# Two wide attentions as one stream of slots, with each group of the input prepared beside the slots before its first use

## The chip, the cores and the metric

The kernel runs on one core of a Trainium2 chip. The core has a matrix engine (TensorE, PE in the rows; PEld is its weight load), three engines for elementwise work (VectorE or DVE, ScalarE or ACT, GpSimd or POOL), SyncE (SP), which issues transfers here, and 16 DMA engines. The metric is the device time of one execution in microseconds, from three runs, and beside it one profiled execution with a trace of all instructions.

## The reference

The input x has 32 x 64 = 2048 tokens of 256 values, and so has the context. Four layers follow one another. The first one, cut to what matters here:

```python
def _cross_attention(q_in, kv_in, wq, bq, wk, bk, wv, bv, wo, bo, bias_k, bias_v):   # H = 16 heads, K = 128
    qh, kh, vh = (q_in @ wq + bq), (kv_in @ wk + bk), (kv_in @ wv + bv)      # each split into heads
    kh = concatenate([kh, bias_k]); vh = concatenate([vh, bias_v])            # one learned key and value
    weights = softmax(einsum('bqhk,bthk->bhqt', qh, kh) / sqrt(K))
    return einsum('bhqt,bthk->bqhk', weights, vh).reshape(...) @ wo + bo

h = layer_norm(x, ln1_scale, ln1_offset);  x = x + _cross_attention(h, ctx, ...1)
h = layer_norm(x, ln2_scale, ln2_offset);  x = x + _cross_attention(h, ctx, ...2)
h = layer_norm(x, ln_mlp_scale, ln_mlp_offset)
x = x + gelu(h @ w_fc1 + b_fc1) @ w_fc2 + b_fc2                               # F = 1024
```

A sequence has 64 queries and 64 keys. The layers after it (a grouped attention, an instance normalised one, a decoder layer with an MLP) are the same code before and after.

## The kernel before

All products of this layer are made in pairs of float32r parts: an operand is split into a high part (a copy rounded to float32r) and a low part (operand minus high part), and `product` (L98 to L102) makes three matmuls, high x high, high x low and low x high.

The tokens are 16 tiles of 128 rows (`NT`), in four groups of four tiles, 512 tokens (`NG`, `GT`, `GN`). `chip.x` holds the rows. `h_hi` and `h_lo` hold the normalised input with the features on the partitions (turned), `ctx_hi` and `ctx_lo` the context.

The stages run one after another, with a barrier between them:

- `load` (L110) brings the context and x in on SP's queue, turns the context on TensorE, splits it (ScalarE, GpSimd), and measures both on VectorE.
- `wide_attention` runs twice (n = 1, 2). It first calls `turn_input` (L186), which for all four groups inverts the spread on GpSimd (L92, L94), normalises the rows on VectorE (L277), turns them (L238), scales them and splits them (L256, L259 on ScalarE, L270 on VectorE). Biases are turned into columns beside it (L364, L369), and `spread_v` is set up for the product of the learned values (L375, L377).
- Then come the slots. One slot is one head for one group: 8 passes of two heads (`HP`) and four groups, 64 slots. A slot n does on TensorE: turn the weights of slot n-1 (L522), project q, context product of slot n-2 (L542), project k and v, for odd slots the output product of a group into `o_ps`, then the scores (L588). ScalarE empties q, k, v, makes the exponential and the high part of the context product (L621 to L648), VectorE makes the softmax and the low part (L667 to L688) and adds `o_ps` to x (L718), GpSimd splits the next pass's weights (L468 to L487). The last pass is written out, the others are one loop body.
- The learned value of each head enters through `learned_weight` (one column a head), which is turned in one go at the end (L528), and multiplied by `value_rows` for all 16 tiles (L567, L706). `value_rows` comes from a product over all heads, `values` (L512), half of it before slot 0 and half behind it.
- The MLP of this layer, `dense_mlp` with tag l0m, loads and splits its weights beside its own `turn_input`, then runs 4 groups of 8 chunks (`FC`): the first layer's chunk f+2, then the second layer's chunk f. From group 1 on it also turns the finished rows for the next layer (L853).

## Time and profile before

| what | value |
|---|---|
| median of 3 runs | 1855.43 us (1854.35 to 1855.84) |
| the profiled execution, its own time | 1856.37 us |
| its span, first to last instruction | 1854.4 us |
| mean granted TensorE clock | 0.959 of full speed |
| busy: TensorE, VectorE, ScalarE, GpSimd | 92, 51, 55, 26% |

### The profile page before, as it was taken

To read this page: it belongs to the slowest core of one execution; us is meant where nothing else is said; L and a number is where in the kernel's file an instruction comes from. 1 tells how busy PE (TensorE), PEld (TensorE's weight loads), DVE (VectorE), ACT (ScalarE), POOL (GpSimd) and SP (SyncE) were. 2 spreads that over 40 slices of the span, in tenths; PEclk is the share of its full clock that TensorE was granted. 3 is DMA by queue.
4 is the path that set the end of the run, shared out by engine and by line. 5 is a ranking of instruction groups with operands and counts; after the bars stand their busy time and mean duration, and the time that the engine had idled before them with its cause. 6 is when DMAs were issued, how large, how long until landed. Compare 5 with 4: busy or idle time off the path is not lost. (4 is left out here: it accounts for less than half of the span.)

```text
span 1854.4 us, 36201 instructions
## 1 busy us (share of the span) xinstructions
PE 1713.5 (92%) x14357; PEld 1458.7 (79%) x14357; DVE 950.7 (51%) x2107; ACT 1012.1 (55%) x1949; POOL 481.3 (26%) x554
## 2 busy tenths in 40 slices
PE   5999999999978999999999869999989889997599
PEld 4888898888867898888888758866766567776598
DVE  6444444444454444444444473467859847668433
ACT  5455555554524555555455434457748857776444
POOL 5000000000012000000000021147764558876411
PEclk7999999999988999999999979989989989999799
DMA  5000000000002000000000020030010000001001
GB/s 160 24 23 9 13 23 23 23 0 23 1 21 72 1 23 23 23 0 23 23 23 0 1 77 1 1 101 2 2 22 2 1 6 2 1 7 36 1 12 34
DMA packets 58100, 39.87 MB, mean 22 GB/s; under 512 B 14693, under 2 KB 57238, under 8 KB 58006
## 3 DMA queue, kind: packets, MB, share of 16 engines
q1 hardware_dynamic: 58006, 38.57, 7.1%
q8 instruction: 65, 1.06, 0.2%
q14 instruction: 29, 0.24, 0.0%
HBM read 36.46 MB, written 2.10 MB: 21 GB/s over the span
## 5 line engine op out<-in xcount | busy, mean ns | idle before, releaser
L679 DVE TENSOR_TENSOR l0a_c_lo<-l0a_c_ps,l0a_c_hi 128x512 fp32r<-128x512 f32 x128 | 88.6, 692 | 267.3 <-ACT l0a_c_hi L633 267.3
L621 ACT ACTIVATE l0a_weight_t<-l0a_t_ps 64x256 f32<-64x256 f32 x256 | 96.9, 378 | 230.7 <-PE l0a_t_ps L522 229.2
L718 DVE TENSOR_TENSOR x<-l0a_o_ps,x 128x1024 f32<-128x1024 f32 x64 | 78.4, 1225 | 202.7 <-PE l0a_o_ps L102 202.7
L542 PEld LDWEIGHTS l0a_c_ps<-l0a_weight_t,l0a_v 128*128 128x128 f32 x1024 | 135.3, 193 | 14.3 <-ACT l0a_weight_t L621 3.0
L468 POOL COPY l0a_head_bias<-l0a_bias_cols 128x2 f32 (+1 forms) x32 | 6.9, 214 | 531.2 <-DVE l0a_logit L672 531.2
L100 PE MATMUL l0a_o_ps<-l0a_wo_hi,l0a_c_hi 128*128 128x256 f32 x512 | 144.2, 282 | 0.0
L101 PE MATMUL l0a_o_ps<-l0a_wo_lo,l0a_c_hi 128*128 128x256 f32 x512 | 143.8, 281 | 0.0
L102 PE MATMUL l0a_o_ps<-l0a_wo_hi,l0a_c_lo 128*128 128x256 f32 x512 | 143.7, 281 | 0.0
L102 PE MATMUL l0a_v_ps<-l0a_wv_hi,ctx_lo 128*128 128x256 f32 x512 | 143.6, 280 | 0.0
L100 PE MATMUL l0a_v_ps<-l0a_wv_hi,ctx_hi 128*128 128x256 f32 x512 | 143.6, 280 | 0.0
L101 PE MATMUL l0a_v_ps<-l0a_wv_lo,ctx_hi 128*128 128x256 f32 x512 | 143.0, 279 | 0.0
L542 PE MATMUL l0a_c_ps<-l0a_weight_t,l0a_v 128*128 128x128 f32 x1024 | 137.1, 277 | 1.7 <-ACT l0a_weight_t L621 1.7
L630 ACT ACTIVATE l0a_q<-l0a_q_ps,l0a_head_bias 128x512 f32<-128x512 f32 x128 | 88.0, 687 | 90.0 <-PE l0a_q_ps L102 89.3
L639 ACT ACTIVATE l0a_k<-l0a_k_ps,l0a_head_bias 128x512 f32<-128x512 f32 x128 | 88.1, 689 | 63.8 <-PE l0a_k_ps L102 63.8
L648 ACT ACTIVATE l0a_v<-l0a_v_ps 128x512 f32<-128x512 f32 x128 | 76.5, 598 | 77.1 <-PE l0a_v_ps L102 77.1
L100 PE MATMUL l0a_q_ps<-h_hi,l0a_w_hi 128*128 128x512 f32 x256 | 112.4, 439 | 3.5 <-POOL l0a_w_lo L473 3.5
L100 PE MATMUL l0a_k_ps<-ctx_hi,l0a_w_hi 128*128 128x512 f32 x256 | 111.3, 435 | 0.0
L102 PE MATMUL l0a_k_ps<-ctx_hi,l0a_w_lo 128*128 128x512 f32 x256 | 101.2, 395 | 0.0
L102 PE MATMUL l0a_q_ps<-h_hi,l0a_w_lo 128*128 128x512 f32 x256 | 101.1, 395 | 0.0
L101 PE MATMUL l0a_q_ps<-h_lo,l0a_w_hi 128*128 128x512 f32 x256 | 100.9, 394 | 0.0
L101 PE MATMUL l0a_k_ps<-ctx_lo,l0a_w_hi 128*128 128x512 f32 x256 | 100.9, 394 | 0.0
L101 PEld LDWEIGHTS l0a_v_ps<-l0a_wv_lo,ctx_hi 128*128 128x128 f32 x512 | 96.0, 187 | 6.0
(429 smaller groups left out, 4869.5 us busy)
## 6 DMA issues: line engine op xcount, KB each, us to landing
l0a_raw<-in_L_xattn_wq_dram SPq DMA_DIRECT2D x32, 128.0 KB, 2.2
l0a_raw<-in_L_xattn_wk_dram SPq DMA_DIRECT2D x32, 128.0 KB, 2.3
l0a_raw_v<-in_L_xattn_wv_dram SPq DMA_DIRECT2D x16, 256.0 KB, 3.0
l0a_raw_o<-in_L_xattn_wo_dram SPq DMA_DIRECT2D x32, 128.0 KB, 2.7
l0a_wo_all<-in_L_xattn_wo_dram SPq DMA_DIRECT2D x2, 2048.0 KB, 8.2
ctx_rows<-in_ctx_dram SPq DMA_DIRECT2D x4, 512.0 KB, 5.9
x<-in_x_dram SPq DMA_DIRECT2D x4, 512.0 KB, 9.8
l3a_room<-in_L_xattn_w_fc_dram SPq DMA_DIRECT2D x2, 1024.0 KB, 6.4
```

The costliest lines, as they stand in the source:

```text
L100: pe.matmul(out, wh, mh, start=start, stop=False)
L101: pe.matmul(out, wh, ml, start=False, stop=False)
L102: return pe.matmul(out, wl, mh, start=False, stop=stop)
L468: pool.tensor_copy(head_bias[p][:], bias_cols[:, BQ:BK + 1, bass.ds(i * HP + p, 1)] .rearrange("p a b -> p (a b)"))
L542: last = pe.matmul(by_tile[:, m, b, :, :], v[(j - HP) // HP % 2][:, m * HB + b, p * K:(p + 1) * K], weight_t[:, m, b, :, :].rearrange("p a ...
L621: last = act.activation(weight_t[half, :, :, a, :], t_ps[half, 0:GT // 2 * P] .rearrange("p (m b q) -> p m b q", b=HB, q=SEQ), ACT.Copy)
L630: act.activation(q[:], q_ps[:], ACT.Identity, bias=head_bias[p][:, 0:1]).then_inc(q_done, 1)
L639: act.activation(k[p][:, :, 0:SEQ], k_ps[:].rearrange("p (b k) -> p b k", k=SEQ), ACT.Identity, bias=head_bias[p][:, 1:2]).then_inc(k_done, 1)
L648: act.activation(v[j // HP % 2][:, p * GT // HP:(p + 1) * GT // HP, :] .rearrange("p t k -> p (t k)"), v_ps[:], ACT.Copy).then_inc(v_done, 1)
L679: dve.tensor_tensor(c[p][1][:], c_ps[:], c[p][0][:].bitcast(F32), ALU.subtract).then_inc(c_lo, 1)
L718: dve.tensor_tensor(chip.x[:, rows, :], o_ps[:], chip.x[:, rows, :], ALU.add).then_inc(added, 1)
```

## The change

`load`, the two `wide_attention` calls and their `turn_input` become one function, `wide_attentions`, with one stream of 128 slots over both attentions. Numbered over both, S = 0 to 127, `passes` writes out S = 0 to 9, loops over passes 1 to 6, writes out the two passes around the seam (S = 58 to 73), loops again and writes out the last.

- x of group 0 and the weights go on SP's queue, the context and x of groups 1 to 3 on ScalarE's. Only group 0 of x and groups 0 and 1 of the context are turned ahead of slot 0. Groups 2 and 3 of the context are turned in slots 0, 2 and 3.
- `TURNS` says at the end of which slot a group of the input is turned (S = 0, 2, 4 for the first attention, 62, 64, 66, 68 for the second, 126 for the MLP's group 0), into `o_ps`. VectorE measures it two slots ahead, GpSimd normalises it one slot ahead, ScalarE and VectorE empty it one slot later and GpSimd makes the low part. Its first use is two slots later.
- The second attention's slots follow the first one's. The product of the learned values is made at the end of slots 8 and 72 in one piece, and `keep_values` one slot later; the learned weights of a group are turned with its last weights and multiplied in its last output product (four fp32 matmuls into `o_ps`).
- The first MLP's weights, biases and gains are fetched on SP's queue during the attentions, behind the second attention's value weights and ahead of pass 2's weights. In the MLP they are split in eight quarters behind the first chunks (`BEHIND`), and its groups 1 to 3 of the input are measured, normalised, turned and split in chunks of the groups ahead (`ENTRY`).
- The stage of the MLP's `turn_input` is gone. `dense_mlp` for the last layer is as before.

The diff, cut to its core:

```diff
-def load(chip):
-def turn_input(chip, tag, scale=None, offset=None, beside=None, bare=False):
-def wide_attention(chip, tag, n):
+def wide_attentions(chip, buffer, gain, mlp):
+    LAST = ATT * PASSES - 1
+    TURNS = {0: 1, 2: 2, 4: 3, **{(PASSES - 1) * ITEMS + 6 + HP * g: NG + g for g in range(NG)}, LAST * ITEMS + 6: 2 * NG}
+    VALUES = {ITEMS: 0, (PASSES + 1) * ITEMS: 1}
+    SPREAD = {HP * HP: 0, ITEMS + 1: 1}
...
+        half_banks = [o_ps[:, HP * x:HP * x + HP, :].rearrange("p t n -> p (t n)") for x in range(CH)]
...
+        def passes(engine, slots):
+            slots(0, 0, True, False, False)
+            slots(0, 1, True, True, False)
+            for j in range(2, ITEMS + 2):
+                slots(0, j, True, True, True)
+            with engine.Fori(1, PASSES - 1) as i:
+                for j in range(2, ITEMS + 2):
+                    slots(i, j, True, True, True)
+            for i in (PASSES - 1, PASSES):
+                for j in range(2, ITEMS + 2):
+                    slots(i, j, True, True, True)
+            with engine.Fori(PASSES + 1, LAST) as i:
+                for j in range(2, ITEMS + 2):
+                    slots(i, j, True, True, True, 1)
+            for j in range(2, ITEMS + 2):
+                slots(LAST, j, j < ITEMS, j <= ITEMS, True)
...
+                def normalise(n):
+                    invert(n)
+                    pool.wait_ge(norm_done, n + 1)
+                    pool.wait_ge(x_turned, n * CH)
+                    for t in range(GT):
+                        at = n % NG * GT + t
+                        pool.tensor_scalar(rows[:, t, :], chip.x[:, at, :], chip.x_moments[:, at, 0:1], norm_inverse[:, t:t + 1],
+                                           ALU.subtract, ALU.mult).then_inc(rows_done, 1)
...
+                    if S is not None and S - 1 in TURNS:
+                        m = TURNS[S - 1]
+                        for ch in range(CH):
+                            pool.wait_ge(x_whole_done, CH * m + ch + 1)
+                            pool.tensor_tensor(chip.h_lo[:, ch, group_columns(m % NG)], whole[:, ch, :],
+                                               chip.h_hi[:, ch, group_columns(m % NG)].bitcast(F32), ALU.subtract).then_inc(x_lo_done, 1)
...
+                        for t in range(GT):
+                            if ending is not None:
+                                last = pe.matmul(o_ps[:, t, :], weights_t[:], value_rows[:, t, :], start=False, stop=True)
...
+                    if S in TURNS:
+                        m = TURNS[S]
+                        if S == 0:
+                            pe.wait_ge(cols_done, 1)
+                        elif S == 2:
+                            pe.wait_ge(x_whole_done, CH * m)
+                        else:
+                            pe.wait_ge(added, outputs_before(S))
+                        turn_rows(m, half_banks)
...
+                act.dma_start(ctx_rows[:, group_rows(0), :], ctx_dram[:, group_rows(0), :]).then_inc(rows_in[0], 16)
+                for x in range(2):
+                    act.dma_start(gain[:, 0, x, :], columns(norms[0][x]), allow_slow_non_contiguous=True).then_inc(gain_in[0], 16)
+                for g in range(1, NG):
+                    act.dma_start(ctx_rows[:, group_rows(g), :], ctx_dram[:, group_rows(g), :]).then_inc(rows_in[g], 16)
+                    act.dma_start(chip.x[:, group_rows(g), :], x_dram[:, group_rows(g), :]).then_inc(x_in[g], 16)
+                for ch in range(CH):
+                    take_context(0, ch)
+                split_w(0, 0)
+                for ch in range(CH):
+                    take_context(1, ch)
+                take_rows(0, first_banks)
+                split_w(0, 1)
+                split_wv(0)
...
+                dve.wait_ge(x_in[0], 16)
+                measure_group(0)
+                for ch in range(CH):
+                    rest_of_context(0, ch)
+                normalise(0)
+                take_biases(0)
...
-def dense_mlp(chip, tag, scale, offset, w1, b1, w2, b2, function, prepared=None, out=None, room=None, turn=None):
+def dense_mlp(chip, tag, function, prepared, out=None, turn=None, entry=None):
+    ENTRY = {0: 3, 1: 1, 2: 1} if entry is not None else {}
...
+            quarters = [quarters[i] for i in (0, 2, 1, 4, 3, 6, 5, 7)]
+            BEHIND = (-1, -1, -1, 0, 1, 2, 3, 4)
+            FIRST_LAYER, SECOND_LAYER = (1, 2, 4, 6), (3, 5, 7, 8)
...
+                    if entry is not None and f == 0 and g > 0:
+                        pe.wait_ge(x_lo_done, CH * g)
+                    if entry is not None and g == 0 and f % QUARTER == 0:
+                        pe.wait_ge(w_lo_done, FIRST_LAYER[f // QUARTER])
```

## Rows read from the trace of the kernel before

**Rows 1.** The page, busy time of TensorE: us, share, instructions, then the other engines.

```profile
PE 1713.5 (92%) x14357; PEld 1458.7 (79%) x14357; DVE 950.7 (51%) x2107; ACT 1012.1 (55%) x1949; POOL 481.3 (26%) x554
```

**Rows 2.** Busy time by stretch: length, each engine's, PEclk, DMA share, GB/s.

```profile
60.00:514.00 454.00, 452.24 (x3720) 405.40 (x3716) 192.27 (x457) 234.26 (x448) 32.31 (x50) 1.00 0.06 16
523.74:573.19 49.45, 30.91 (x138) 25.33 (x134) 32.47 (x85) 15.09 (x25) 11.99 (x19) 0.72 0.22 65
1056.19:1101.16 44.97, 24.89 (x117) 20.41 (x114) 33.03 (x77) 13.98 (x24) 9.16 (x10) 0.70 0.16 50
0.00:40.73 40.73, 20.81 (x86) 17.55 (x86) 28.44 (x98) 21.41 (x35) 26.17 (x37) 0.75 0.58 182
```

**Rows 3.** Timeline of PE, first slots: start, us, what, records.

```profile
45.84 3.72 PE L512 MATMUL l0a_o_ps<-l0a_wo_all,l0a_spread_v 128*128 128x256 f32 x16
49.21 0.58 PE L100 MATMUL l0a_q_ps<-h_hi,l0a_w_hi 128*128 128x512 f32 x1
...
54.31 0.44 PE L522 MATMUL l0a_t_ps<-ident,l0a_weight 128*128 128x128 f32 x2
...
60.41 0.44 PE L522 MATMUL l0a_t_ps<-ident,l0a_weight 128*128 128x128 f32 x2
...
69.35 0.44 PE L522 MATMUL l0a_t_ps<-ident,l0a_weight 128*128 128x128 f32 x2
```

**Rows 4.** Timeline of PE, between the two attentions.

```profile
538.91 1.03 PE L567 MATMUL l0a_k_ps<-l0a_value_rows,l0a_weights_t 128*128 128x256 f32 x4
539.78 1.03 PE L567 MATMUL l0a_v_ps<-l0a_value_rows,l0a_weights_t 128*128 128x256 f32 x4
...
586.77 0.44 PE L522 MATMUL l0a_t_ps<-ident,l0a_weight 128*128 128x128 f32 x2
```

**Rows 5.** Timeline of PE, first MLP.

```profile
1111.16 0.40 PE L100 MATMUL l0m_hidden_ps<-h_hi,l0m_w_hi 128*128 128x512 f32 x1
...
1146.80 1.03 PE L853 MATMUL l0m_turn_ps<-ident,x 128*128 128x128 f32 x8
1147.59 0.47 PE L100 MATMUL l0m_hidden_ps<-h_hi,l0m_w_hi 128*128 128x512 f32 x1
```

**Rows 6.** Timeline of DVE, start and end of the attentions.

```profile
4.54 1.41 DVE L178 BATCH_NORM_STATS2 ctx_stats<-ctx_rows 128x6 f32<-128x256 f32 x4 [4.54 <-DMA ctx_rows<-in_ctx_dram]
...
36.51 1.34 DVE L657 TENSOR_TENSOR l0a_wv_lo<-l0a_raw_v,l0a_wv_hi 128x512 fp32r<-128x512 f32 x1 [2.02 <-ACT l0a_wv_hi L608]
...
53.12 1.77 DVE L698 TENSOR_TENSOR l0a_value_rows<-l0a_o_ps,l0a_bo_rows 32x256 f32<-32x256 f32 x4
...
59.33 0.16 DVE L688 TENSOR_TENSOR l0a_learned_weight<-l0a_expd,l0a_inverse 128x4 f32 x1
...
1065.41 0.69 DVE L679 TENSOR_TENSOR l0a_c_lo<-l0a_c_ps,l0a_c_hi 128x512 fp32r<-128x512 f32 x1 [4.33 <-ACT l0a_c_hi L633]
...
1079.14 1.23 DVE L718 TENSOR_TENSOR x<-l0a_o_ps,x 128x1024 f32<-128x1024 f32 x1 [0.38 <-PE l0a_o_ps L102]
1080.40 1.41 DVE L76 BATCH_NORM_STATS2 x_stats<-x 128x6 f32<-128x256 f32 x4
1082.87 1.17 DVE L83 BATCH_NORM_AGGREGATE x_moments<-x_stats 128x2 f32<-128x6 f32 x16 [1.07 <-PEq L65]
```

**Rows 7.** Groups by line: busy us, mean ns, idle before (whole span, then 0:110).

```profile
L473 POOL TENSOR_TENSOR l0a_w_lo<-l0a_raw,l0a_w_hi 128x512 fp32r<-128x512 f32 x32 | 40.8, 1274 | 73.2 <-ACT l0a_w_hi L603 73.2
...
L2281 POOL TENSOR_SCALAR l_normed<-l3a_room,ctx_moments,ctx_inverse 128x256 f32<-128x256 f32 x14 | 17.4, 1246 | 23.0 <-PE l_conv_ps L2226 23.0
...
L277 DVE TENSOR_SCALAR l0a1h_rows<-x,x_moments,l0a1h_inverse 128x256 f32<-128x256 f32 x16 | 8.2, 576 | 0.9 <-POOL l0a1h_inverse L94 0.7
...
L256 ACT ACTIVATE h_hi<-l0a1h_turned,l0a1h_gain 128x512 fp32r<-128x512 f32 x8 | 6.3, 788 | 7.7 <-PE l0a1h_turned L238 7.7
...
L94 POOL TENSOR_TENSOR l0a1h_inverse<-l0a1h_spread,minus_half 128x4 f32<-128x4 f32 x4 | 4.8, 1196 | 0.3
```

**Rows 8.** Timeline of SP's DMA issues, window 7:9.2: start, us of the issue.

```profile
6.56 2.52 SPq L133 DMA_DIRECT2D x<-in_x_dram  x1
```

More of the change, by code:

```diff
@@ new lines, in _ @@
+                next_pass(1)
+                fetch_pass(0, [(HP + p) * K for p in range(HP)])
+                sp.wait_ge(values_done, 1)
+                fetch_values(1)
+                sp.wait_ge(ctx_turned, CH * NG)
+                sp.wait_ge(ctx_gathered, NG)
+                mlp["sync"](sp)
+                with sp.Fori(2, PASSES) as i:
+                    starts = [sp.snap((i * HP + p) * K) for p in range(HP)]
+                    ends, count = sp.snap(i * HP), sp.snap(i * 1)
+                    sp.wait_ge(w_split, ends)
+                    sp.wait_ge(wv_split, count)
+                    sp.wait_ge(wo_split, count)
+                    fetch_pass(0, starts)
@@ L177, in _, with measure_group @@
+                def measure_group(m):
+                    g = m % NG
+                    for t in range(GT):
+                        measure(chip, dve, g * GT + t).then_inc(measured, 1)
+                    dve.wait_ge(measured, GT * (m + 1))
                     for t in range(g * GT, (g + 1) * GT):
-                        dve.bn_stats(stats[:, t, :], rows[:, t, :]).then_inc(stats_done, 1)
+                        last = dve.bn_aggr(chip.x_moments[:, t, :], chip.x_stats[:, t, :])
+                    last.then_inc(gathered, 1)
@@ new lines, in normalise, with take_whole @@
+                def normalise(m):
+                    dve.wait_ge(norm_done, m + 1)
+                    if m > 0:
+                        dve.wait_ge(x_turned, CH * m)
+                    for t in range(GT):
+                        at = m * GT + t
+                        dve.tensor_scalar(rows[:, t, :], chip.x[:, at, :], chip.x_moments[:, at, 0:1], norm_inverse[:, t:t + 1],
+                                          ALU.subtract, ALU.mult).then_inc(rows_done, 1)
+                def take_whole(m, ch, bank):
+                    norm = m // NG
+                    dve.wait_ge(x_hi_done, CH * m + ch + 1)
+                    if m > 0:
+                        dve.wait_ge(x_lo_done, CH * (m - 1) + ch + 1)
+                    dve.tensor_scalar(whole[:, ch, :], bank[:], gain[:, norm, 0, ch:ch + 1], gain[:, norm, 1, ch:ch + 1],
+                                      ALU.mult, ALU.add).then_inc(x_whole_done, 1)
@@ L191, in turn_input @@
+                split_wv(0)
+                dve.wait_ge(x_in[1], 16)
+                measure_group(1)
+                normalise(1)
+                dve.wait_ge(zeroed, 4)
+                passes(dve, slots)
+    chip.end_stage()
+def dense_mlp(chip, tag, function, prepared, out=None, turn=None, entry=None):
     nc = chip.nc
-    scaled_norm = scale is not None
-    norm = scaled_norm or bare
-    beside = beside or {}
+    LEAD = 2
+    ENTRY = {0: 3, 1: 1, 2: 1} if entry is not None else {}
@@ L781, in dense_mlp @@
-        if not prepared:
-            with ExitStack() as before:
-                prepare(before)
+            w_hi_done, w_lo_done = sem("w_hi_done"), sem("w_lo_done")
+            QUARTER = 2
+            quarters = []
+            for start in range(0, FC, QUARTER):
+                cols, own = slice(start * P, (start + QUARTER) * P), slice(start, start + QUARTER)
+                quarters += [(raw1[:, :, cols], w1_hi[:, :, cols], w1_lo[:, :, cols]), (raw2[:, own, :], w2_hi[:, own, :], w2_lo[:, own, :])]
@@ L845, in first, with turn_entry @@
                     last.then_inc(hidden_made, 1)
+                def turn_entry(n):
+                    if n >= 2:
+                        pe.wait_ge(turned_lo, CH * (n - 1))
+                    for c in range(CH):
+                        for j in range(GT):
+                            if c == 0:
+                                pe.wait_ge(rows_done, n * GT + j + 1)
+                            last = pe.transpose(turn_ps[:, c, j * P:(j + 1) * P], rows[n % 2][:, j, c * P:(c + 1) * P], chip.ident[:])
+                        last.then_inc(x_turned, 1)
                 def turn_rows(g):
@@ L857, in group @@
                     for f in range(FC):
+                        if entry is not None and ENTRY.get(g) == f:
+                            turn_entry(g)
                         if turn and f == 5 and g > 0:
```

1183 lines of the change are left out of this document (600 added, 583 removed).

## The prediction

> **What bounds the kernel now.** I read the page first: TensorE is busy for 92% of the span [rows 1], so outside its own work there are some 140 us to be had. Where they lie I read from the busy time by stretch. In 454 us in the midst of the first attention TensorE is busy for 452.24, at a granted clock of 1.00; in the three stretches around the attentions it is busy for 20.81 of 40.73, 30.91 of 49.45 and 24.89 of 44.97 us, at clocks of 0.75, 0.72 and 0.70 [rows 2]. What looks busy there is partly slow: at the lower of the two clock levels a matmul takes twice its time. So the attention slots are bound by TensorE, and the three stretches by chains over the other engines. The change fills the stretches with slots.
>
> The timeline of TensorE then gives the unit. A slot is one head for one group of 512 tokens. An even slot takes 60.41 - 54.31 = 6.10 us, an odd one (with the output product) 69.35 - 60.41 = 8.94, a pair 15.04 [rows 3]. Counted in slots over both attentions (S), S=2 starts at 54.31, S=64 would start at 523.74 and S=128 at 1056.19, where the second and third stretch begin [rows 2, 3]; S=66 (slot 2 of the second attention) starts at 586.77 [rows 4], chunk 1 of the MLP at 1111.16 [rows 5]. I compare before and after at these marks.
>
> **Prices used.** A turn of one group (8 transposes), warm: 1147.59 - 1146.80 = 0.79 us [rows 5]. Learned product: four records, that is two matmuls, are 539.78 - 538.91 = 0.87 us apart, so 0.43 a matmul, 1.74 for a group's four; with its one more transpose (0.1) 1.84 [rows 4]. Values product: half of it takes 49.21 - 45.84 = 3.37 us, all of it 6.74 [rows 3].
>
> **Stretch 1, start to S=2.** Before, nothing useful starts until everything is loaded, measured, normalised, turned and split. After, only group 0 is. The chain: x of group 0 and the first context rows land at about 5.5 us (two 512 KB transfers share what one had, whose first use is at 4.5 [rows 6]). ScalarE is the question, since it now issues nine DMAs, seven of them of 512 KB, before its first activation. On SP the last of eight such issues was held until 6.56 + 2.52 = 9.08 us, an issue that lasted 2.52 us where half a microsecond is what one of these takes unheld [rows 8]; the queue takes some four large transfers and then holds its issuer. Three of ScalarE's seven must land first, beside 1.5 MB on SP, 3 MB in all. At SP's rate, (eight less four held) x 0.5 MB in 9.08 - 2.2 us, at least 300 GB/s, ScalarE is free at 10.5 us. Bounds: 5.5 (never held) and 14.3 (held until all is in).
> From there: two context copies of ScalarE 1.0 (two thirds of the 0.79 of its scaled 128x512 pass, an estimate), VectorE's two rests 1.3, normalise 4 x 0.53 (16 take 8.2 us busy), turn at the lower clock 1.8 of which 0.7 is behind the last row, ScalarE's two 128x512 of 0.79, VectorE's whole and low parts, four of about 0.7 [rows 6, 7]: 10.5 + 1.0 + 0.7 + 2.1 + 0.7 + 1.3 + 2.5 = 18.8 us for the first q. Slot 0 is half at the lower clock, with two turns 8.3 us, slot 1 is 5.1 and waits 0.4 for the context of group 2: S=2 at 32.6, against 54.31. That is 21.7 us less (bounds 18 to 26).
> Of what is moved into slots there are two more turns of x and one of context, 2.4; the values, 6.74; and slot 9 waits for the kept values: VectorE does them after the weights, which are ready 5.0 us into a slot (the learned column ends the series), in 1.77 us [rows 6], against TensorE's wish for o_ps at 5.6: 1.2. Together 10.3. **Net -11.4 us.**
>
> **Stretch 2, S=64 to S=66.** Before 586.77 - 523.74 = 63.03 us. After: one pair 15.04, values and their wait 7.9, four turns 3.2, four learned products 7.4 (in slots 59 to 65): 33.5. **Net -29.5 us.**
>
> **Stretch 3, S=128 to MLP chunk 1.** Before 1111.16 - 1056.19 = 54.97 us. After, the drain keeps its first part, to c_lo at 1065.41 + 0.69 [rows 6], 0.6 earlier as three learned transposes are gone. Then 24 output matmuls and one learned product, 4.6 us warm and up to 9 at the lower level; the stretch's clock of 0.70 [rows 2] says partly: 6.4. The add is 1.23, and from the end of the last statistics, which are gone, to the next stage's first aggregation are 1082.87 - 1081.81 = 1.1 [rows 6]. New stage at 1074.4. A weight quarter (128x512) has its high part from ScalarE in some 0.7 and its low part from VectorE in 0.7: first hidden product at 1075.9, then 12 matmuls mostly at the lower clock (4.6), 1.4 for chunk 2's, 1.4 for the first output product: chunk 1 at 1083.2 on before's axis, 28.0 earlier. Back: three learned products and one turn inside the slots 6.3, three turns in the MLP 2.4, and 1.0 for VectorE in chunks 2 to 4 (a chunk is 2.8 us; low, weight quarter, and four statistics with their aggregation are 0.7 + 0.7 + 1.7 = 3.1, against some 2.7 us of lead; bounds 0 to 4). **Net -18.3 us.**
>
> **What is costed at nothing.** *GpSimd* now normalises: a 128x256 tensor_scalar takes 1.246 us there, the pow 1.2, a 128x512 subtraction 1.27 [rows 7]. A turn costs it 0.23 + 1.2 + 4 x 1.25 = 6.4 and later 2.5. In an odd slot it ends the low parts about 5.0 us in, and the next normalisation 6.4 later, 2.5 us into the even slot; TensorE turns there from 5.4 on. So 2.9 us of slack. In slot 64 it also has the second head's weights, ready 6.4 us in, needed at 6.9: half a microsecond. *ScalarE* gets 1.3 us in slots S+1 and copies a learned tile: all are odd slots of 8.9 us; q and k are done by 5.0, and the scores ask for them after 8. *VectorE* ends a measuring even slot 0.7 late, and the exponential waits behind c_hi anyway. *SP*: 4 MB of values and MLP weights go ahead of pass 2's weights, 12 to 14 us; from slot 9 to their use in slot 15 are 45 us. Late next, if its cover goes, is the turn, and with it q of the next slot.
> The row shows a subtraction of two SBUF operands on VectorE of 1.34 us beside a GpSimd one, where 0.69 is usual for this shape [rows 6, 7]. In this case's stream only the weights' 0.43 us product has two SBUF inputs; a held one would be late by up to 1.25, on nine turns 11 us; by the time at which GpSimd is at work (2.5 to 11.4 us after an odd slot's start) it falls in odd slots, whose 3 us of spare hold it. The Trainium skill, "SBUF — State Buffer", "Who interferes with whom", has a VectorE instruction with two SBUF inputs wait out a GpSimd instruction that reads SBUF, for its whole length. By that rule, the trace agrees: 1.34 against 0.69. By it the sum would be 4 us less of a gain, in the MLP, where the low parts of chunks 1 to 4 run beside GpSimd's normalisation.
>
> **Sum.** -11.4 - 29.5 - 18.3 = -59.2. The profiled execution took 1856.4 us, 2.0 beyond its span, and 0.9 over the median of 1855.4. 1856.4 - 59.2 = 1797.2; by the median 1796.2. I predict 1797. Bounds: start -4 to +4, drain clock -2 to +2, MLP -1 to +4, weights' product 0 to +11.
>
> **Rivals.**
> 1. *GpSimd comes late and each turn waits.* For: 1.25 us a row tile, and half-microsecond cover in slot 64. Against: 2.9 us of slack. If its work stretches to twice the time, as the row of 1.34 has it for the other engine, low parts end at 7.5 and rows at 20.3 us, against 14.3: 6 us on each of the five turns that follow another, 30 in all: about 1827.
> 2. *The start is not limited by DMA issue* (free at 5.5 us) and the clock is up early everywhere: -4 - 2 - 1: 1790. Within my range; its far end, with slot 0 warm, is 1785.
> 3. *The other side: instruction supply.* The change writes out 34 slots where 20 were. If TensorE waited in each written-out slot for code, 59.2 / 34 = 1.75 us a slot would eat the gain, and from there it is slower than before: at 2.0 us a slot 1797 + 68 = 1865. Against it, slots 58 to 63 are written out today, and S=64's mark comes at 523.74, 62 slots or 31 pairs of 15.04 (466.2) and eight loop turns after 54.31: 469.4, no wait to be seen.
> 4. *It does not do what it says:* a chain outside of TensorE holds each group as now, within 0.2% of 1855. Nothing but a semaphore that I misread could do this.
>
> **Chances.** Forecast (1785 to 1813) 0.82, rival 1 (1813 to 1850) 0.12, rival 2's far end under 1785 0.03, rival 3 0.02, rival 4 0.01. Leaving out 2 in 10, the range is 1787 to 1813. Below 0.2% (3.7 us, about what a measurement can tell from no change): faster 0.97, same 0.01, slower 0.02.
>
> **What would show it.** Right: the first q at 17 to 21 us; S=2 at about 33; no stretch between the attentions where TensorE's clock falls; 33.5 us where 63.0 were; values' second half without a break; turns of 0.8 us inside slots. Wrong: idle time of TensorE in slots 1 to 6 or 60 to 70 put down to the normalised rows or the low parts of h (rival 1), to nothing that the profile shows (rival 3); ScalarE's first copy at 6 or at 14 us; MLP chunks 2 to 4 longer than 2.8 us.

## The result and the profile after

The changed kernel takes 1800.83 us (median of 3 runs, 1799.94 to 1801.93), the kernel before 1855.43: ratio 0.9707, 95% interval 0.9685 to 0.9729. Forecast was 1797, range 1787 to 1813; the point was 3.8 us too low. The profiled execution has a span of 1799.1 us, against 1854.4, so the trace shows 55.3 us less where the sum said 59.2.

The page of the kernel after, busy time of the engines [rows 1]:

```profile
PE 1689.8 (94%) x14356; PEld 1444.5 (80%) x14356; DVE 938.7 (52%) x2064; ACT 995.4 (55%) x1932; POOL 545.7 (30%) x601
```

Busy time by stretch, kernel after. The cuts are the starts of slots 2, 10, 58, 64, 66, 74, 122 and 128 and of chunk 1 of the MLP; columns as in [rows 2]:

```profile
0.00:36.14 36.14, 20.23 (x125) 17.21 (x126) 22.84 (x53) 13.24 (x21) 15.56 (x29) 1.00 0.70 206
36.14:108.37 72.23, 70.79 (x558) 63.49 (x558) 41.23 (x128) 34.86 (x66) 23.88 (x23) 1.00 0.19 60
108.37:471.52 363.15, 361.70 (x2981) 325.02 (x2977) 154.08 (x367) 188.54 (x360) 26.78 (x42) 1.00 0.07 21
471.52:522.96 51.44, 51.44 (x412) 45.67 (x408) 24.55 (x64) 24.71 (x49) 14.86 (x16) 1.00 0.07 22
522.96:540.68 17.72, 17.72 (x146) 15.80 (x142) 10.41 (x27) 9.76 (x19) 12.46 (x13) 1.00 0.01 2
540.68:611.10 70.42, 68.97 (x549) 62.03 (x545) 32.57 (x78) 33.88 (x64) 17.37 (x19) 1.00 0.05 16
...
974.23:1025.67 51.44, 51.44 (x411) 45.66 (x408) 22.15 (x56) 24.23 (x48) 10.17 (x9) 1.00 0.00 1
1025.67:1053.39 27.72, 17.89 (x87) 14.97 (x84) 11.14 (x29) 10.34 (x19) 3.95 (x4) 0.75 0.20 49
```

The seam is the row to look at: from slot 64 to slot 66 TensorE is busy for all of 17.72 us at a granted clock of 1.00; before, the same two slots took 63.03 us and the clock fell to 0.72 [rows 2]. (The 1.00 of the first row is not to be trusted, see the last section.) The drain into the MLP is what is left at a low clock, 0.75 over 27.72 us.

Timeline of PE, kernel after: first turns, first q, slot 2, slot 9's wait, the seam, the MLP [rows 3 to 5].

```profile
6.70 1.09 PE L396 MATMUL l0a_c_ps<-ident,l3a_room 128*128 128x128 f32 x4 [6.70 <-DMA l3a_room<-in_ctx_dram]
...
13.54 0.71 PE L410 MATMUL l0a_o_ps<-ident,l0a_bias_rows 16*128 16x16 f32 x5 [4.90 <-DMA l0a_bias_rows<-in_L_xattn_bias_v_dram]
...
15.95 1.06 PE L404 MATMUL l0a_s_ps<-ident,l0a_rows 128*128 128x128 f32 x4
...
21.23 0.76 PE L81 MATMUL l0a_q_ps<-h_hi,l0a_w_hi 128*128 128x512 f32 x1 [3.37 <-issue]
...
36.14 0.44 PE L433 MATMUL l0a_t_ps<-ident,l0a_weight 128*128 128x128 f32 x2 [0.94 <-DVE ctx_lo L661]
...
104.75 0.36 PE L81 MATMUL l0a_o_ps<-l0a_wo_hi,l0a_c_hi 128*128 128x256 f32 x1 [1.44 <-DVE l0a_value_rows L704]
...
522.96 0.44 PE L433 MATMUL l0a_t_ps<-ident,l0a_weight 128*128 128x128 f32 x2
...
529.04 1.09 PE L404 MATMUL l0a_o_ps<-ident,l0a_rows 128*128 128x128 f32 x8
529.97 0.38 PE L433 MATMUL l0a_t_ps<-ident,l0a_weight 128*128 128x128 f32 x2
...
540.68 0.44 PE L433 MATMUL l0a_t_ps<-ident,l0a_weight 128*128 128x128 f32 x2
...
1053.39 0.40 PE L81 MATMUL l0m_hidden_ps<-h_hi,l0m_w_hi 128*128 128x512 f32 x1
...
1086.40 0.50 PE L81 MATMUL l0m_hidden_ps<-h_hi,l0m_w_hi 128*128 128x512 f32 x1 [3.07 <-ACT l0m_hidden L1002]
```

To compare stretch by stretch, two more marks of the kernel before are needed, the starts of slots 58 and 122; the third row is its one wait inside the MLP. Timeline of PE, kernel before:

```profile
478.66 0.44 PE L522 MATMUL l0a_t_ps<-ident,l0a_weight 128*128 128x128 f32 x2
...
1011.11 0.44 PE L522 MATMUL l0a_t_ps<-ident,l0a_weight 128*128 128x128 f32 x2
...
1141.00 0.50 PE L100 MATMUL l0m_hidden_ps<-h_hi,l0m_w_hi 128*128 128x512 f32 x1 [1.48 <-ACT l0m_hidden L905]
```

The cuts at 58 and 122 put the learned products where the forecast counted them:

| stretch | before | after | measured | forecast |
|---|---|---|---|---|
| 1: start to slot 58 | 478.66 | 471.52 | -7.1 | -11.4 |
| 2: slot 58 to slot 122 | 532.45 | 502.71 | -29.7 | -29.5 |
| 3: slot 122 to the end | 843.29 | 824.87 | -18.4 | -18.3 |
| sum | 1854.4 | 1799.1 | -55.3 | -59.2 |

Two of the three stretches came out as worked, and the miss lies in the first; stretch 3 did so because deviations of 2 to 3 us cancel in it, as shown further down. So the experiments are about the start, about the places where TensorE still waits for more than 1 us outside the start and the drain (104.75, its twin in slot 73, and 1086.40), and about the rivals.

The other engines of the kernel after, for what follows. Timeline of ACT (issues are ACTq rows):

```profile
4.70 2.18 ACTq L624 DMA_DIRECT2D x<-in_x_dram  x1
...
9.19 1.59 ACTq L624 DMA_DIRECT2D x<-in_x_dram  x1
10.81 1.28 ACT L561 ACT_TABLE_LOAD   x1 [10.81 <-issue]
12.11 0.60 ACT L561 ACTIVATE ctx_hi<-l0a_c_ps 128x512 fp32r<-128x512 f32 x1
...
1084.12 0.31 ACT L1925 ACTIVATE l1a_wv_hi<-l1a_raw_v 128x128 fp32r<-128x128 f32 x1 [5.22 <-DVE l1a_set_k L1915]
```

Timeline of DVE:

```profile
13.95 2.23 DVE L670 TENSOR_SCALAR l0a_rows<-x,x_moments,l0a_norm_inverse 128x256 f32<-128x256 f32 x4
...
24.95 3.73 DVE L670 TENSOR_SCALAR l0a_rows<-x,x_moments,l0a_norm_inverse 128x256 f32<-128x256 f32 x4 [1.49 <-POOL l0a_norm_inverse L328]
...
102.84 1.77 DVE L704 TENSOR_TENSOR l0a_value_rows<-l0a_o_ps,l0a_bo_rows 32x256 f32<-32x256 f32 x4
...
1054.93 0.68 DVE L1063 TENSOR_TENSOR l0m_w_lo<-l3a_room,l0m_w_hi 128x512 fp32r<-128x512 f32 x1
...
1060.75 2.90 DVE L1063 TENSOR_TENSOR l0m_w_lo<-l3a_room,l0m_w_hi 128x512 fp32r<-128x512 f32 x1
...
1079.71 2.53 DVE L1910 COPY l1a_set_q<-l1a_raw_q 128x256 f32<-128x256 f32 x2
```

Timeline of POOL:

```profile
24.87 0.95 POOL L386 MEMSET l0a_value_rows<- 128x1024 f32 x1
25.76 1.81 POOL L387 MEMSET l3a_room<- 128x2048 f32 x1
...
521.21 5.39 POOL L336 TENSOR_SCALAR l0a_rows<-x,x_moments,l0a_norm_inverse 128x256 f32<-128x256 f32 x4
...
528.40 1.28 POOL L320 TENSOR_TENSOR l0a_w_lo<-l0a_raw,l0a_w_hi 128x512 fp32r<-128x512 f32 x1 [1.54 <-ACT l0a_w_hi L552]
...
1050.71 7.13 POOL L870 TENSOR_SCALAR l3a_room<-x,x_moments,l0m_norm_inverse 128x256 f32<-128x256 f32 x4
...
1060.17 2.92 POOL L887 TENSOR_TENSOR x<-x,l0m_b_row 128x1024 f32<-128x1024 f32 x1
```

### The profile page after: what moved, and what is told of

Read it like the earlier page. It is cut to its first block and busy times, and to the rows that moved or that the text cites. A ratio compares the mean times of both kernels' runs of the same rounds, so it can differ in the third digit from the quotient of the medians.

```text
span 1799.1 us, 36043 instructions
## 1 busy us (share of the span) xinstructions
PE 1689.8 (94%) x14356; PEld 1444.5 (80%) x14356; DVE 938.7 (52%) x2064; ACT 995.4 (55%) x1932; POOL 545.7 (30%) x601
## 5 line engine op out<-in xcount | busy, mean ns | idle before, releaser
L81 PE MATMUL l0a_o_ps<-l0a_wo_hi,l0a_c_hi 128*128 128x256 f32 x512 | 149.3, 292 | 4.3 <-DVE l0a_value_rows L704 2.9
L81 PEld LDWEIGHTS l0a_o_ps<-l0a_wo_hi,l0a_c_hi 128*128 128x128 f32 x512 | 97.0, 189 | 5.8 <-issue 3.2
L81 PEld LDWEIGHTS l0a_v_ps<-l0a_wv_hi,ctx_hi 128*128 128x128 f32 x512 | 96.2, 188 | 6.0
```

The lines of the kernel that those rows point to most:

```text
L81: pe.matmul(out, wh, mh, start=start, stop=False)
```

## The experiments

Eleven kernels, each the changed kernel with one edit, or several together where it says so. Times are medians; the runs of the kernel before in the three groups of runs had medians of 1854.88, 1855.33 and 1855.82 us. A difference of about 1 us between two of them is the limit of what the medians tell (the changed kernel has 1800.83), so the marks in the traces carry the small ones.

### The start: which chain sets the first q

The forecast had one chain, through ScalarE's held DMA issues. The trace has a second: TensorE stands until 13.54 for the bias rows, and behind that, in its order, come the second context group and the rows of x. Five runs are about the two. For reading them: from the turn of the bias rows to the first q are 7.69 us in the changed kernel, and what matters is whether that distance stays. In the runs that leave the start alone, further down, the bias rows are turned at 13.20 to 13.42 and the first q comes at 20.89 to 21.10, so 0.4 us of the first q differs from one execution to the next.

**A table load hidden behind the issues.**

```diff
+                act.wait_ge(ident_set, 1)
+                act.activation(early[:], chip.one[:], ACT.Copy)
                 for g in range(1, NG):
                     act.dma_start(ctx_rows[:, group_rows(g), :], ...
```

> One added activation of 128x1 on ScalarE, behind its first three DMA issues, so that the activation table is loaded while the queue holds it. Theory A (the start is a chain through ScalarE: DMA issues until 10.78 us, table load of 1.28 us, first copy at 12.11): the first copy is at 10.8 to 11.0, the first q at 20.0 instead of 21.23, slot 2 at 34.9 instead of 36.14, the total 1.2 us lower (1799.6). Rival B (the chain runs through TensorE, which waits for the bias rows until 13.54 us): first q and total unchanged within 0.4 us, because the second context half is turned only at 14.19 to 15.95 whatever ScalarE does.

Measured: 1800.88 us, ratio 0.9709 (0.9693 to 0.9725). ScalarE's first copy came at 11.05 instead of 12.11, and nothing followed from it. Timeline of PE in this run:

```profile
13.61 0.71 PE L411 MATMUL l0a_o_ps<-ident,l0a_bias_rows 16*128 16x16 f32 x5 [4.90 <-DMA l0a_bias_rows<-in_L_xattn_bias_v_dram]
...
21.30 0.61 PE L81 MATMUL l0a_q_ps<-h_hi,l0a_w_hi 128*128 128x512 f32 x1 [3.37 <-issue]
```

The first q is at 21.30 against 21.23, again 7.69 us behind the bias rows. Rival B is right and Theory A falls: in the changed kernel ScalarE isn't on the path, the bias rows are.

**Rows of x normalised before the first context rests.**

```diff
+                normalise(0)
                 for ch in range(CH):
                     rest_of_context(0, ch)
-                normalise(0)
```

> VectorE normalises group 0 of x before it takes the low parts of the first context group, nothing else. The inverse is ready at 9.33 us, so the rows are ready at 11.6 instead of 16.2. Theory A (chain through ScalarE and VectorE's rows): TensorE still turns biases at 13.54 and the second context group until 15.95, and the rows' turn at 15.95 no longer waits; first q about 20.9 to 21.2, gain 0 to 0.4 us in all. If the rows were what the turn waited for most, the gain would be up to 2.2 us. Rival B (TensorE's wait for the bias rows sets all that follows) also says 0 to 0.4, so this run only bounds the rows' share.

Measured: 1801.26 us, 0.971 (0.9694 to 0.9727). The rows are ready at 10.8 us (four passes in 1.38 us from 9.40), 5.4 us earlier, TensorE still turns the biases at 13.26, first q 20.95: 0.3 us earlier, as much as the biases landed earlier, and inside what executions differ by. By itself the edit gives nothing.

**Five of ScalarE's seven large loads issued by SP, behind the first weights.**

```diff
-                for g in range(1, NG):
-                    act.dma_start(ctx_rows[:, group_rows(g), :], ...   # and x
+                act.dma_start(ctx_rows[:, group_rows(1), :], ...
...
+                for g in range(1, NG):                                 # on SP, behind fetch_o
+                    if g > 1:
+                        sp.dma_start(ctx_rows[:, group_rows(g), :], ...
+                    sp.dma_start(chip.x[:, group_rows(g), :], ...
```

> ScalarE issues only the context groups 0 and 1 and the gains; the other five 512 KB loads are issued by SP behind the first pass's weights. Theory A (ScalarE held by its own issues is what starts the work late): ScalarE is free at 3.5 us, its table load is hidden, first context copy at about 7.7 us instead of 12.11; then TensorE's bias rows are next, which land earlier too, with less ahead of them (8 to 10 us). First q at 17 to 18 us instead of 21.23, total 3 to 4 us lower (1797 to 1798). Rival B (the bias rows bound it, and they land when the large transfers ahead are through, about 13.5 us, as before): first q at 20.5 or later, total at most 0.7 us lower.

Measured: 1801.17 us, 0.9705 (0.9689 to 0.9722). ScalarE is free at 3.4 us and its first copy is at 7.95, 4.2 us earlier; TensorE waits 3.8 us for the bias rows instead of 4.9 and turns them at 12.52, the first q comes 7.69 us later at 20.21, and slot 2 starts at 35.10 against 36.14. Theory A had 3 to 4 us. Taking the hold away moves the start by 1.0, and it does so through the bias rows, which land 1.0 earlier with fewer of ScalarE's loads beside them; the median shows none of it.

**Only the bias rows ahead of the weights.**

```diff
                 sp.dma_start(chip.x[:, group_rows(0), :], ...
+                fetch_biases(0)
                 fetch_w(0, slice(0, K), 0)
...
-                fetch_biases(0)
```

> Only the five bias rows fetched ahead of the first weights. Theory (two chains of nearly one length lead to the first q: the bias rows through TensorE, and ScalarE's held issues with the table load through VectorE's rows; cutting one alone gives nothing): TensorE turns the biases at about 9, the second context group by 10.8 to 12, yet VectorE's rows are ready at 16.2 as before, so the first q is at 20.5 to 21.3 and the total within 0.8 us of 1800.8. Rival (the bias rows alone set the first q): first q at 17 to 18, total 3 us lower.

Measured: 1799.45 us, 0.9699 (0.9684 to 0.9714). Timeline of PE:

```profile
8.75 0.71 PE L410 MATMUL l0a_o_ps<-ident,l0a_bias_rows 16*128 16x16 f32 x5
...
12.54 1.12 PE L404 MATMUL l0a_s_ps<-ident,l0a_rows 128*128 128x128 f32 x3 [1.18 <-DVE l0a_rows L670]
14.46 0.48 PE L404 MATMUL l0a_s_ps<-ident,l0a_rows 128*128 128x128 f32 x1 [0.80 <-DVE l0a_rows L670]
...
19.16 0.77 PE L81 MATMUL l0a_q_ps<-h_hi,l0a_w_hi 128*128 128x512 f32 x1 [3.37 <-issue]
```

The wait for the DMA is gone and a wait for VectorE's rows stands in its place, 1.18 + 0.80 us: there is the chain through ScalarE. But the first q is 2.1 us earlier, not 0 to 0.7 as my theory had it, and the total 1.4 lower. ScalarE was free at 8.95 instead of 10.78 and its first copy came at 10.24, 1.87 us earlier, which brought VectorE's rows forward too. So this run moved both chains, and it doesn't say what the order of the bias rows is worth alone; by the difference of 2.07 and 1.87 an estimate is 0.2 us. That fits the changed kernel's own trace, where VectorE's last row is ready at 16.18 (13.95 + 2.23) and TensorE turns it at 16.59: ScalarE's chain was only 0.4 us from being the later one. Why the held issues got shorter when 40 KB of biases moved ahead was not found.

**All three together.**

> Loads on SP as in the run before, the five bias rows fetched ahead of the weights, and group 0 of x normalised before the first context rests. Theory A: context copies at 7.7, bias rows at 7 or so, rows normalised 9.35 to 11.6, turned by 12.3, ScalarE's and VectorE's four passes of 3.2 us: first q at 15 to 16.5 us instead of 21.23, slot 2 at 30 to 31.5 instead of 36.14, total 1795 to 1796. Rival C (bandwidth: what is needed first lands no earlier however it is issued): first q at 19 or later, total above 1798.

Measured: 1796.63 us, 0.9686 (0.967 to 0.9702). Timeline of PE:

```profile
8.82 0.71 PE L414 MATMUL l0a_o_ps<-ident,l0a_bias_rows 16*128 16x16 f32 x5
...
16.53 0.77 PE L81 MATMUL l0a_q_ps<-h_hi,l0a_w_hi 128*128 128x512 f32 x1 [3.39 <-DVE h_lo L783]
...
31.44 0.44 PE L437 MATMUL l0a_t_ps<-ident,l0a_weight 128*128 128x128 f32 x2 [0.94 <-DVE ctx_lo L663]
```

First q at 16.53, slot 2 at 31.44: 4.7 us earlier than 21.23 and 36.14, more than the parts give alone. The bias rows are turned at 8.82, 4.72 us earlier and right behind the first context group, with no wait left there, and the first q follows 7.71 us later: now no part of either chain stretches the distance. Rival C falls: the data were there. In the total 4.2 us of it are seen; by the first product of the MLP the lead was 3.7, since the drain before it took 21.6 us from slot 128 here and 20.6 in the changed kernel.

### The two waits that are left

**The kept rows.** In slots 9 and 73 VectorE adds the output bias to the values product behind the attention weights; TensorE's output product waits for it.

```diff
+                    if S is not None and S - 1 in VALUES:    # right behind the shifted logits
+                        keep_values(VALUES[S - 1])
...
-                    if S is not None and S - 1 in VALUES:    # behind the learned weights
-                        keep_values(VALUES[S - 1])
```

> VectorE keeps the four rows of the values product right behind the shifted logits of slots 9 and 73, ahead of the low parts of the head product. Theory A (the two waits of 1.44 us for the kept rows come from their place behind the weights in VectorE's order): both waits go; slots 9 and 73 take 8.9 to 9.2 us instead of 10.56; total 2.5 to 2.9 us lower (1798.1). Rival B (a wait takes its place: the low parts of the head product or the weights, 1.77 us later, hold TensorE): the slots stay above 10.2 us, total within 0.7 us of 1800.8.

Measured: 1797.86 us, 0.9692 (0.9676 to 0.9708). Timeline of DVE: the four additions now lie ahead of the low parts of the head product, in time in which VectorE stood idle for TensorE.

```profile
97.68 1.78 DVE L704 TENSOR_TENSOR l0a_value_rows<-l0a_o_ps,l0a_bo_rows 32x256 f32<-32x256 f32 x4 [5.64 <-PE l0a_o_ps L533]
100.83 0.69 DVE L732 TENSOR_TENSOR l0a_c_lo<-l0a_c_ps,l0a_c_hi 128x512 fp32r<-128x512 f32 x1 [1.37 <-ACT l0a_c_hi L598]
```

VectorE still waits 1.37 us for ScalarE behind them, so nothing was made late. The two slots got 1.67 and 1.68 us shorter (8.88 instead of 10.55 and 10.57). Theory A holds.

**The next stage's weights inside the MLP.** In group 1, chunk 2, ScalarE splits four weights of the next attention, and stands until VectorE has ordered two of them.

```diff
-                            if g == 1 and f == 2:
+                            if g == 1 and f == 4:
                                 hooks["scalar"](act)
```

> In the first MLP ScalarE splits the next stage's four weights behind chunk 4 of group 1 instead of chunk 2; VectorE orders them where it did. Theory A (TensorE's one wait of 3.07 us in the MLP, at 1086.40, comes from ScalarE standing for VectorE's copies, which ended at 1084.2): ScalarE no longer stands, hidden chunks follow at 2.8 us, the wait goes or shrinks to under 1 us, total 2 to 3 us lower (1798 to 1799). Rival B (VectorE itself is late: its low parts of the hidden tiles queue behind the same copies until 1084.2): TensorE waits at the output product instead, gain under 1 us.

Measured: 1796.54 us (1794.5 to 1799.08), 0.9681 (0.9664 to 0.9697). In its trace the only waits of TensorE inside the MLP's groups are two of 0.2 us for low parts of hidden tiles. What that is worth is read inside the MLP: from the start of chunk 1 to its last output product it takes 90.5 us here and in the run of all edits, and 93.3 to 93.4 in five traces that keep the wait of 3.07 us and go on at full clock behind it (the loads on SP, the biases first and all three together; the rows kept early; GpSimd's work twice), so 2.9 us. In the changed kernel and three others (the table load, the rows first, the loop written out) it takes 94.3 to 94.9, because there the clock fell behind the wait. The chunk behind it in the changed kernel, and the same chunk in the run with the rows kept early (columns as above):

```profile
1086.40:1090.86 4.46, 4.46 (x19) 3.97 (x20) 1.39 (x2) 2.50 (x4) 3.66 (x3) 0.62 0.00 0
...
1083.83:1086.76 2.93, 2.93 (x19) 2.52 (x19) 1.39 (x2) 2.40 (x4) 2.93 (x3) 1.00 0.00 0
```

TensorE had been idle for 3.07 us in both, and lost 1.5 us more at a granted clock of 0.62 in one. So the edit gives 2.9 us, and 4.4 against a trace in which the clock fell; the stages behind the MLP, which run the same code, took 2.1 us longer in this trace than in the changed kernel's, and the single times of this run scatter by 4.6. Theory A holds: ScalarE stood, VectorE's own lateness was covered by the lead of two chunks. Timeline of DVE in this run, the two low parts that had waited for the copies:

```profile
1084.05 1.27 DVE L1040 TENSOR_TENSOR l0m_hidden_lo<-l0m_hidden,l0m_hidden_hi 128x512 fp32r<-128x512 f32 x2
```

### The rivals and the terms

**GpSimd's slack (rival 1).**

```diff
+                        pool.tensor_scalar(twice[:], chip.x[:, at, :], chip.x_moments[:, at, 0:1], norm_inverse[:, t:t + 1], ...)
                         pool.tensor_scalar(rows[:, t, :], chip.x[:, at, :], chip.x_moments[:, at, 0:1], norm_inverse[:, t:t + 1], ...)
```

> GpSimd computes every normalised row tile of the stream twice, the first into a tile that nobody reads: 4.9 us more for each of eight turns. Theory A (the turns have slack: rows end at 41.0, 56.1, 526.6, 542.2 and 559.7 us where TensorE turns them from 42.2, 59.4, 529.0, 546.8 and 562.6): waits of 3.4, 1.6, 2.2, 0.3 and 1.9 us, 0.9 more behind the turn of slot 64, where the next head's weights queue behind them on GpSimd, none at slots 62 and 126: 10 us more, 1811 (1808 to 1813). Rival (GpSimd already sets the pace of the turns): 4.9 us on at least five turns, 1825 or more. Rival (GpSimd doesn't matter): within 1 us of 1800.8.

Measured: 1813.48 us, 0.9774 (0.9758 to 0.9791). Timeline of PE: turns that wait for rows, and the q behind that of slot 64.

```profile
43.45 0.33 PE L409 MATMUL l0a_o_ps<-ident,l0a_rows 128*128 128x128 f32 x1 [0.91 <-POOL l0a_rows L339]
45.86 1.33 PE L409 MATMUL l0a_o_ps<-ident,l0a_rows 128*128 128x128 f32 x5 [2.08 <-POOL l0a_rows L339]
...
537.50 0.77 PE L409 MATMUL l0a_o_ps<-ident,l0a_rows 128*128 128x128 f32 x5 [2.02 <-POOL l0a_rows L339]
...
539.00 0.50 PE L81 MATMUL l0a_q_ps<-h_hi,l0a_w_hi 128*128 128x512 f32 x1 [0.40 <-POOL l0a_w_lo L321]
...
573.34 0.77 PE L409 MATMUL l0a_o_ps<-ident,l0a_rows 128*128 128x128 f32 x5 [1.36 <-POOL l0a_rows L339]
```

By the marks against the changed kernel, slot 2 is 4.4 us longer, slot 3 1.7, slot 64 2.2, slots 65 and 68 0.7 and 1.6, slot 128 comes 10.4 us later and the MLP's first product 11.2; 10 was expected, and the total is half a microsecond above the expected range. (The expectation spoke of eight turns; GpSimd normalises for seven, VectorE for the one of slot 0.) So 34 us of added work cost 11 to 13. What was not foreseen is slot 3: no wait stands in it, but it ran at a granted clock of 0.82, its first records at 0.63 us for 0.39, behind a stretch in which TensorE was busy for 2.3 of 4.8 us. GpSimd wasn't the bound, and the slack is what it looked like, 1.2 us at slot 2 and 2.4 to 4.6 at the others, with the next head's weights behind it in slot 64.

**Instruction supply (rival 3).**

```diff
-            with engine.Fori(1, PASSES - 1) as i:
-                for j in range(2, ITEMS + 2):
-                    slots(i, j, True, True, True)
-            for i in (PASSES - 1, PASSES):
+            for i in range(1, PASSES + 1):
                 for j in range(2, ITEMS + 2):
                     slots(i, j, True, True, True)
```

> The loop over passes 1 to 6 of the first attention is written out on the four engines: 48 more slots as straight code, 82 instead of 34. Theory A (instruction supply costs nothing in written-out slots; what was seen in 34 holds): pairs stay at 15.0 us, total within 1.5 us of 1800.8, perhaps 1 us lower as the 0.5 us at each pass of the loop goes. Rival 3 of the prediction (each written-out slot waits for code): at 0.5 us a slot 24 us more, 1825; at its price of 1.75 us a slot 84 us more, 1885.

Measured: 1800.52 us, 0.9705 (0.9688 to 0.9721). Slots 2, 58 and 128 start within 0.15 us of where they do in the changed kernel. 48 more written-out slots cost nothing that can be measured, so rival 3 has no price here.

**The moved products.**

```diff
-                            if ending is not None:
-                                last = pe.matmul(o_ps[:, t, :], weights_t[:], value_rows[:, t, :], start=False, stop=True)
...
-                        for h in range(H):
+                        for h in range(1):
                             last = pe.matmul(o_ps[:, 0, :], spread_v[:, h, :], wo_all[:, h, :], ...)
```

> Leaves out 15 of the 16 products of the learned values in both attentions and all products of the learned weights with them (four a group, 32 in all); transposes, copies and kept rows stay. Theory A (what was moved into the slots costs TensorE its full time there, since TensorE is the bound): 2 x 6.6 + 32 x 0.43 = 27 us less than 1800.8, 1774 (1772 to 1776). Rival (part of it lies in time that TensorE would wait for other engines anyway): 20 us less or fewer, 1781 or more.

Measured: 1776.84 us, 0.9575 (0.956 to 0.959): 24.0 us less than 1800.8, between the two expectations. The marks say more. The 15 products of the values took 6.5 us of each of slots 8 and 72, the learned products 1.72 us of each of the seven slots in which they lay, and the MLP's first product comes 26.1 us earlier, against 27. So in the stream the moved work costs its full time; in the trace 2.7 us were given back behind that product, in stages that run the same code. Those stages took 752.8 us in the changed kernel, 752.1 to 755.2 in the runs that did not touch them, and 755.5 here; 1.5 of the 2.7 lie in the MLP, where the clock was low for 6.8 us twice instead of 3.4. Whether the edit has a part in that is open.

**The edits together.** Loads on SP, biases and rows first, rows kept early, the split behind chunk 4.

> The edits of four earlier runs together: loads on SP, bias rows first and rows of x first at the start; kept rows early; the split of the next stage's weights behind chunk 4. Theory A (three separate waits on the one path): the gains add, 4.2 + 2.9 + 4.3 = 11.4 us below 1800.8, 1789.4 (1788 to 1791). Rival (they share slack, one takes another's place): 1792 or more.

Measured: 1790.41 us (1789.54 to 1793.11, 5 runs), 0.9652 (0.9639 to 0.9665). Slot 2 is 4.65 us earlier, slot 74 7.95 (3.3 of it in slots 9 and 73), the end 10.4. The waits were separate and the gains add, to within the microsecond that the expectation was too large. It is the fastest version found, 10.4 us under the changed kernel.

## Why the prediction was right, and where its size was off

**The sum, 3.9 us too large by the spans.** Most of it is one term: "Stretch 1, start to S=2", first q at 18.8 us; it came at 21.23, which is 2.4 us of the miss. The mechanism was held to be "ScalarE is the question". Its size came out near (free at 10.5 forecast, 10.78 measured), but partly by luck: the working had three of ScalarE's loads landed and 3 MB through from time 0 at 300 GB/s, and the trace has two landed (6.56 and 10.76) and 2.5 MB through by 10.78, at a mean of 236 GB/s. And it was not what set the first q. The bias rows did: SP's queue delivers them behind 1.25 MB of x and weights, in the bandwidth that ScalarE's loads take too, at 13.5 us, and TensorE's order puts them ahead of the second context group and the rows. The prediction never listed that wait. The first three runs show it: with the copy 1.06 us earlier, the rows 5.4 earlier, or ScalarE free 7.4 earlier, the first q stayed 7.69 us behind the bias rows. ScalarE's own chain was about 0.4 us behind: also unlisted were the table load of 1.28 us at its head, and 2.23 us for four normalisations beside a GpSimd subtraction against 1.38 by themselves.

**Slots 0 and 1** were forecast at 13.8 us and took 14.9, 1.1 more. Half of it is slot 0, 8.9 instead of 8.3 us with no wait in it to speak of. The other half is the wait for the context of group 2, 0.94 us (0.4 forecast): VectorE's rows for group 1 took 3.73 us beside two GpSimd memsets, and its product of the weights, a little ahead of that low part, 1.31 us instead of 0.43 beside a GpSimd subtraction, with VectorE hardly idle in between.

**Back in the slots, stretch 1:** from slot 2 to slot 10 the kernel takes 72.23 us against 60.63, 11.6 back where 10.3 was worked out. Each part is a little larger: the kept wait 1.44 us and 1.67 for the slot (1.2 forecast), a turn 0.93 inside a slot (7.01 of slot 64 less 6.08), not 0.79, the values 7.01, not 6.74. The other way, each of the six loop passes up to slot 58 got 0.1 us shorter, which was not counted.

**Stretch 2** was right to 0.2 us, partly since small errors cancel: values with their wait 8.7 instead of 7.9, turns 3.7 instead of 3.2, learned products 7.3 instead of 7.4, and against them 1.4 us of shorter pairs and loop passes. The essential step, that TensorE finds each of group 0 to 3 turned and split when it comes to it, is the row 522.96:540.68, with no idle time in it.

**Stretch 3:** the drain and the start of the MLP took 27.72 us (27.0 forecast, bounds 25 to 29), the products inside the slots 6.36 (6.3). "1.0 for VectorE in chunks 2 to 4" was wrong in place: those chunks took 3.57 us (with a turn of 0.8), 2.90 and 2.81, with no wait. What came instead is at 1086.40, where the existing wait of 1.48 us grew to 3.07, because VectorE reaches its copies later (two passes for the turned group, 1.5 us, are ahead of them) and one of them took 1.38 us instead of 0.28 beside GpSimd. This is the piece costed at nothing that lost its cover, at 1.6 us, and behind it the clock fell for 3.4 us, 1.5 us more that no term of the sum had. From chunk 1 to its last output product the MLP so took 94.9 us against 89.6 before, 5.3 more where 3.4 was forecast. That the whole stretch still came out right is luck: the stages behind the MLP, which run the same code, took 650.9 us in this trace against 653.7 in that of before, and 650.7 to 654.5 in the others.

**What was costed at nothing.** GpSimd: rows ended 2.4 us (slot 64) and 4.5 us (slot 66) before their turn, where 2.9 was forecast; the half microsecond in slot 64 is 529.68 (528.40 + 1.28) against q at 530.21, 0.53 us. VectorE's weights' product was held in seven slots of 128, 0.72 to 0.79 us instead of 0.43 in six of them, inside the 3 us of spare, and 1.31 in slot 1, where it has its part in the wait of 0.94; so its bound of 11 us was not touched. SP's values landed long before slot 8.

**The weighed rule.** In the MLP VectorE's low parts of the weights read two SBUF operands. Three of them lie wholly beside GpSimd's four normalisations of 1050.71, which read one such operand: they took 0.68 to 0.69 us, no longer than elsewhere, and it was GpSimd that stretched, 7.13 us where the stream has 4.85 to 5.39. Beside GpSimd's addition of two SBUF operands at 1060.17 the same VectorE instruction took 2.90 us: it started at 1060.75 and ended 0.55 after the addition did, as if it had waited it out. In this trace every VectorE instruction of this kind, 128x512 with two SBUF operands, that starts inside a GpSimd tensor_tensor of 128x512 or 128x1024 ends 0.55 us behind it (two more begin at 1065.00 and 1066.37, 1.30 and 1.65 us long), and none that starts inside a normalisation of GpSimd takes over 0.70. The Trainium skill, "SBUF — State Buffer", "Who interferes with whom", makes no such difference between GpSimd instructions that read SBUF; by its rule all of them would have been held, and the 4 us less of a gain that the forecast worked out from it did not come.

**The rivals.** 1 (GpSimd late) is refuted by the trace and by the doubled run: even with the normalisations done twice the total is 1813, not 1827. 2 (start not limited by DMA issue, 1785 to 1790) is half true in a way I had not seen: with the issues moved away alone, 1801.2; with the biases and the rows moved too, 1796.6, which is still above 1790. 3 (instruction supply) is refuted with 82 written-out slots. 4 did not happen.

## What to carry to other kernels

When a start is shortened, list for each instruction of TensorE's order there what it waits for and when that lands, small transfers too: the one chain that looks long hides the next, and here three cuts of which one gave nothing and the others 1.0 and 2.1 us alone gave 4.7 together. When a stretch of the forecast comes out right to 0.1 us, look inside it all the same: here 2 us more in the MLP and 2.8 us less in untouched stages lay behind it. A transfer of 8 KB queued behind 1.2 MB is as late as the megabyte. After a seam is closed, go through the waits that TensorE still has and ask which engine's own order makes them: two were undone by moving a few lines, 5 us or more together, with no work less.

## What the runs showed of the hardware

- Five transfers of 8 KB, queued on SP at 4.40 to 7.0 us behind 1.25 MB, had landed at 13.5 us beside ScalarE's loads; issued ahead of the weights they had landed by 8.75.
- An activation table load took 1.28 us each of the four times in the trace of the kernel after. In the run with one activation placed between DMA issues the first of them cost ScalarE nothing: ScalarE's queue went on issuing at 2.52 while the load ran from 2.46 to 3.74. The Trainium skill, "ScalarE: Activation LUTs", "What ACT_TABLE_LOAD costs", has 1283 ns for the load, as here, and 1380 more for a drain; the trace does not agree: the next activation begins 0.01 us behind the load at 10.81 and 0.38 behind the one at 1164.22.
- Four VectorE normalisations of 128x256 take 1.38 us alone, 2.23 beside a GpSimd subtraction and 3.73 beside two GpSimd memsets that read nothing (the first of the four 2.76, to 0.14 us behind the second memset's end); a VectorE subtraction of two SBUF operands of 128x512 took 0.66 to 0.70 us in all places where it began inside a GpSimd tensor_scalar of 128x256, and ended 0.55 us behind a GpSimd tensor_tensor of 128x512 or more in all places where it began inside one.
- The page's column gives a granted clock of 1.00 for the first 36 us of the kernel after, but the first q's record is 0.76 us where the same one is 0.48 later: in this stretch the durations tell the level, the column does not.
- The drain, at a granted clock of 0.75, is not the same in each run: from slot 128 to the MLP's first product the traces have 20.2 to 21.7 us with the same code, so more than a microsecond of what the start gains or loses may be gone there.
- The same idle time of 3.07 us of TensorE in the MLP was followed by a fall of the granted clock in five traces (3.4 us at the lower level in four of them, 6.8 in the run without the learned products) and by none in five others; the fall of 3.4 us cost 1.5.
